# Context handed over transposed, half of the masks copied into PSUM by ScalarE, and a reordered rotary fill in a four-layer transformer kernel

## The chip, the core and the metric

The kernel runs on one core of one Trainium2 chip. The metric is the device time of one execution in microseconds (us). TensorE is called PE in the rows (PEld is its weight load), VectorE DVE, ScalarE ACT, GpSimd POOL; SyncE (SP) issues most DMAs.

## The reference, cut to what matters

`x` is [8, 256, 256] (8 sequences of 256 rows, 256 features), `ctx_1024` has the same shape. 16 heads of 16 features.

```python
def _layernorm(x): ...                      # no gain, no shift
x = x + tanh(g0) * L0_xattn(_layernorm(x), ctx, masks)   # two attention blocks
x = x + tanh(f0) * L0_ffn(_layernorm(x))                 # 8 experts, top 2
x = x + tanh(g1) * L1_xattn(_layernorm(x), ctx, keymask) # rotary cross attention
x = x + tanh(f1) * L1_ffn(_layernorm(x))                 # 8 experts, top 1

def mha(q, k, v, ..., mask):                # in L0_xattn: self, then on ctx
    att = Q @ K^T
    att = where(mask == 0, -1e9, att)
    att = softmax(att)
    return (att @ V) @ wo + bo
def L1_xattn(x, ctx):
    q, k, v = x @ Wq + bq, ctx @ Wk + bk, ctx @ Wv + bv
    q, k = rotary(q), rotary(k)
    return softmax(q @ k^T / 8 + keymask) @ v @ Wo + bo
```

## The kernel before, in words

The program has five stages, each a block of five instruction queues, one per engine, with all order between engines kept by semaphores: `prepare` (masks), `attention_pipeline` (both L0 attention blocks), `feed_forward_and_experts`, and `rotary_and_experts` (rotary attention, and its experts).

**Attention pipeline.** A unit `m` is one sequence in one of the two blocks: `m` = 0 to 7 is self attention, 8 to 15 attends to the context (`cross(m)`). The stage runs in beats `b` from -4 to 16, each of 16 slots `h`. In slot `h` of beat `b` PE computes the transposed scores of head `h` of unit `b` (`scores_T`, L523), the plain scores of a later head (`scores`, L505, from which DVE takes the row maxima in `maxima`, L761) and one task of another unit: queries in slot 0, keys in 4, value projection in 8, output projection in 12 (eight matmuls each), the product with V in 1, 5, 9 and 13 (`values`), small transposes in 3, 6, 7, 10, 11 and 15. In slot 14 of beats 4 to 11 `turn_context` (L468) transposes 256 rows of the context with four matmuls against the identity, and ScalarE copies the result to `cT` (`bring_context`, L612). Keys and values of a cross unit are made from `cT`.

Transposed scores use two PSUM banks, T0 for even heads and T1 for odd ones. Per head `scores_T` waits until ScalarE has taken the exponentials out of that bank two heads ago, and then issues three matmuls:

```python
pe.wait_ge(exp_done, H * m + h + 1)
nc.tensor.matmul(dst[:, :], identb[:, :], masks[m // B][1][:, :], start=True, stop=False)   # L528
for u in range(NU):                                                                         # L530
    ins = nc.tensor.matmul(dst[:, u * SEQ:(u + 1) * SEQ], KS[...], QS[...], start=False, stop=(u == NU - 1))
```

The first writes the mask (512 columns, bf16) into the bank, the others add the scores. ScalarE then runs `exps` (L646), an exponential of 128 x 512 from PSUM into `PT`. Between these, ScalarE's queue holds, in the order of the slots: `first_part` and `second_part` (queries and keys are split into three bf16 parts; GpSimd makes the remainders), `keys`, three copies of transposes, and `outputs`.

**Rotary stage.** It opens with a fill, written out by hand per engine, before its first beat. For units 0, 1, 2: transposed context, keys, values, transposed rows, queries; each result passes through one of two shared PSUM banks A and B in the order of the tuple `FILL` and is released by the engine that reads it. DVE multiplies by cosine and sine and leaves two halves in `fk`/`tk` or `fq`/`tq` (`turned`, L1786). GpSimd adds the halves (`whole`, L1632, 1635), and then ScalarE and GpSimd split the sum in turns (L1493, L1640, L1498, L1645). SP writes the parts to DRAM (`spread_parts`, L1080) and reads them back as stacked heads (`stack`, L1069) with the key mask. The rows `x` of a sequence need a layer norm first: DVE takes moments (L114, L118), GpSimd an inverse square root in 14 small steps (`inverse_roots`, L134 to L141), DVE scales (L151).

SP's order: rows of sequence 0, context 0, `wk`, `bk`, two key tables, `wv`, `bv`, the key mask `mcu` (2048 elements of one byte), `wq`, `bq`, two query tables, context 1 and 2, the constant stack rows, then all other `x`. DVE's order: memset of `V`, moments 0, keys 0, norm 0, moments 1, queries 0, keys 1, norm 1, queries 1, keys 2. Unit 2's rows and queries come in the last beat of the fill, b = -1, between the maxima of 8 + 16 heads. Then beat 0 starts with `scores_T(0, 0)` (L1241), which waits for the maxima of unit 0 that SP copies into `QS` (`max_to_queries`, L1084, 1085). In beats 0 to 3, slot 14, the context of unit b + 4 is transposed here too (L1181).

## Time and profile before

| | us |
|---|---|
| median of 3 runs | 1367.42 (1365.85 to 1368.43) |
| the profiled execution's own time | 1368.68 |
| its span, first to last instruction | 1366.9 |
| PE busy | 1199.9 (88%) |
| DVE / ACT / POOL busy | 781.0 / 569.9 / 556.7 |
| from the first `scores_T` of the attention pipeline to its last | 72.2 to 435.4 |
| rotary fill: first DMA issue to first `scores_T` | 887.2 to 964.6 |

Busy time of PE contains the latency of pipelined matmuls: of two that start 0.22 us apart each is shown as 0.38 us long. What one costs in a full queue is the distance between starts.

### The profile page before, as it was taken

The numbers are of one execution on the slowest core, as the hardware profiler recorded it, in microseconds if no ns is written. First come the engines' busy times: TensorE is split into PE (matmuls) and PEld (weight loads), VectorE is DVE, ScalarE is ACT, GpSimd is POOL, SyncE is SP. The second block draws the span as 40 slices with busy tenths as digits, with TensorE's granted clock in tenths as the row PEclk, the third lists the DMA queues.
The fourth block names the chain that finished last, engine by engine and source line by source line (L and its number), as shares of the span: only waits on it lengthen the run. The fifth ranks groups of instructions, "written<-read, shape, count | busy, mean of one in ns | idle before, by whom it ended". The sixth has DMA issues, their size and how long they took to land. (4 is left out here: it accounts for less than half of the span.)

```text
span 1366.9 us, 27489 instructions
## 1 busy us (share of the span) xinstructions
PE 1199.9 (88%) x8469; PEld 968.4 (71%) x8524; DVE 781.0 (57%) x2994; ACT 569.9 (42%) x1404; POOL 556.7 (41%) x927
## 2 busy tenths in 40 slices
PE   4599999999998999899999999447888868689996
PEld 3367677777755788789999999434556645689995
DVE  4587777777773378865333333136787876532231
ACT  2156566666655223233333333112455545233331
POOL 3334454453534235545333333144554433433331
PEclk9799999999999999999999999876899999799998
DMA  4766664635420991123222222187453695511110
GB/s 107 167 139 161 140 162 101 121 84 110 101 48 2 304 285 33 47 30 46 32 40 40 36 37 35 17 188 162 105 105 86 144 279 186 186 33 46 40 35 6
DMA packets 116679, 137.66 MB, mean 101 GB/s; under 512 B 25627, under 2 KB 102953, under 8 KB 111628
## 3 DMA queue, kind: packets, MB, share of 16 engines
q1 hardware_dynamic: 101304, 106.73, 33.1%
q0 software_dynamic: 15232, 29.17, 9.3%
q8 instruction: 72, 1.18, 0.4%
q14 instruction: 71, 0.58, 0.2%
HBM read 102.51 MB, written 35.97 MB: 101 GB/s over the span
## 5 line engine op out<-in xcount | busy, mean ns | idle before, releaser
L768 DVE CUSTOM_DVE_ANT_0 att_masked_scores<-att_S,Bm 128x256 bf16<-128x256 f32 x512 | 192.4, 419 | 66.9 <-PE att_S L511 52.8
L648 ACT ACTIVATE att_PT<-att_T 128x512 f32<-128x512 f32 x256 | 151.4, 595 | 86.3 <-PE att_T L530 77.6
L2432 ACT ACTIVATE moe_hT<-moe_H,moe_b 128x128 f32<-128x128 f32 x312 | 89.2, 369 | 170.1 <-PE moe_H L2345 168.9
L2357 PE MATMUL moe_Z<-moe_W,moe_hT 128*128 x624 | 141.6, 380 | 0.8 <-DVE moe_z L2657 0.8
L2520 POOL DMA_INDIRECT x<-Y,X x39 | 63.7, 1634 | 154.7 <-DVE Y L2668 150.4
L2357 PEld LDWEIGHTS moe_Z<-moe_W,moe_hT 128*128 128x128 f32 x624 | 115.5, 190 | 15.5 <-issue 1.2
L511 PE MATMUL att_S<-L_KS,L_QS 96*128 96x256 bf16 x512 | 99.7, 277 | 18.3 <-DMA L_KS<-att_k_dram 13.3
L530 PE MATMUL att_T<-L_QS,L_KS 99*128 99x256 bf16 x512 | 98.6, 273 | 4.6 <-issue 2.1
L2345 PEld LDWEIGHTS moe_H<-moe_aT,ff_w 128*128 128x128 f32 x832 | 96.8, 192 | 4.0 <-issue 2.1
L2345 PE MATMUL moe_H<-moe_aT,ff_w 128*128 128x128 f32 x832 | 97.2, 275 | 2.3 <-DVE X L2652 1.7
L1805 DVE TENSOR_REDUCE out_mx<-out_S 128x2 f32<-128x512 f32 x128 | 85.1, 684 | 24.6 <-PE out_S L1223 24.0
L2657 DVE TENSOR_TENSOR moe_z<-moe_Z,moe_b 128x256 f32<-128x256 f32 x39 | 16.5, 424 | 141.8 <-PE moe_Z L2357 141.8
L1551 ACT ACTIVATE X<-out_T,L_b 128x128 f32<-128x128 f32 x184 | 52.5, 369 | 98.1 <-PE out_T L1352 97.7
L1352 PEld LDWEIGHTS out_T<-out_xT,L_w1s 128*128 128x128 f32 x736 | 87.2, 195 | 4.4 <-issue 1.8
L1352 PE MATMUL out_T<-out_xT,L_w1s 128*128 128x128 f32 x736 | 87.9, 279 | 2.6 <-DVE L_w1s L1946 1.4
L1517 ACT ACTIVATE L_W<-out_T 128x512 f32<-128x512 f32 x128 | 72.5, 596 | 34.0 <-PE out_T L1241 33.5
L1365 PE MATMUL out_S<-L_W,X 128*128 x368 | 83.5, 380 | 2.4 <-DVE out_ys L1955 2.4
L530 PEld LDWEIGHTS att_T<-L_QS,L_KS 99*128 99x128 bf16 x512 | 50.6, 99 | 38.6 <-issue 0.6
L528 PE MATMUL att_T<-BmT,identb 128*128 128x512 bf16 x201 | 77.2, 384 | 0.4
L1365 PEld LDWEIGHTS out_S<-L_W,X 128*128 128x128 f32 x368 | 68.1, 190 | 11.8 <-issue 3.5
L511 PEld LDWEIGHTS att_S<-L_KS,L_QS 96*128 96x128 bf16 x512 | 48.3, 98 | 32.6 <-DMA L_KS<-att_k_dram 14.2
L1223 PE MATMUL out_S<-L_W 97*128 97x256 bf16 x256 | 52.8, 293 | 21.1 <-DVE out_mx L1805 13.1
(455 smaller groups left out, 2527.1 us busy)
## 6 DMA issues: line engine op xcount, KB each, us to landing
moe_W<-in_L_ffn_W SPq DMA_DIRECT2D x16, 1024.0 KB, 13.6
L_W<-in_L_ffn_W POOLq DMA_DIRECT2D x12, 1024.0 KB, 10.7
att_q_dram<-att_pq SPq DMA_DIRECT2D x16, 384.0 KB, 4.5
att_k_dram<-att_pk SPq DMA_DIRECT2D x16, 384.0 KB, 2.8
L_QS<-att_q_dram SPq DMA_DIRECT2D x16, 384.0 KB, 4.9
L_KS<-att_k_dram SPq DMA_DIRECT2D x16, 384.0 KB, 8.1
L_QS<-att_q_dram SPq DMA_DIRECT2D x16, 256.0 KB, 5.6
L_KS<-att_k_dram SPq DMA_DIRECT2D x16, 256.0 KB, 8.5
```

The source lines that it names most:

```text
L511: ins = nc.tensor.matmul(bankS[h % 2][:, u * SEQ:(u + 1) * SEQ], QS[0:ROWS, m % 3, h, u * P:(u + 1) * P], KS[0:ROWS, m % 3, h, :], start=T ...
L528: nc.tensor.matmul(dst[:, :], identb[:, :], masks[m // B][1][:, :], start=True, stop=False)
L530: ins = nc.tensor.matmul(dst[:, u * SEQ:(u + 1) * SEQ], KS[0:ROWS_ALL, m % 3, h, u * P:(u + 1) * P], QS[0:ROWS_ALL, m % 3, h, :], start=Fa ...
L648: nc.scalar.activation(PT[:, h % 8, :], bankT[h % 2][:, :], ACT.Exp).then_inc(exp_done, 1)
L768: ins = nc.vector.tensor_tensor_reduce(masked_scores[:, h % 2, u, :], bankS[h % 2][:, u * SEQ:(u + 1) * SEQ], masks[m // B][0][:, u * SEQ: ...
L1352: ins = nc.tensor.matmul(bankH[half][:, f * P:(f + 1) * P], matrix[:, cc, k * P:(k + 1) * P], xT[:, s % 2, cc * P:(cc + 1) * P], start=(cc ...
L1365: ins = nc.tensor.matmul(bankY[:, 0:D], eT[:, s % 2, f * P:(f + 1) * P], matrix[:, f, :], start=(f == 0), stop=(f == NF - 1))
L1517: nc.scalar.activation(PT[h % 8], bankT[h % 2][:, :], ACT.Exp).then_inc(exp_done, 1)
L1805: nc.vector.tensor_reduce(mx[:, m % 2, :, h:h + 1], bankS[h % 2][:, :].rearrange("p (u k) -> p u k", u=NU), AXX, ALU.max).then_inc(max_don ...
L2345: ins = nc.tensor.matmul(bankH[half][:, f * P:(f + 1) * P], matrix[:, cc, g * P:(g + 1) * P], xT[:, s % 2, cc * P:(cc + 1) * P], start=(cc ...
L2357: ins = nc.tensor.matmul(bankZ[:, 0:D], eT[:, s % 2, f * P:(f + 1) * P], w2e[:, f, :], start=(f == 0), stop=(f == NF - 1))
L2432: ins = nc.scalar.activation(eT[:, s % 2, g * P:(g + 1) * P], bankH[half][:, f * P:(f + 1) * P], ACT.Relu, bias=b1[:, bass.ds(e * NF + g, 1)])
```

## The change

Three things change together.

1. The host hands over `ctx_1024` with its last two axes exchanged. `turn_context`, `bring_context`, `cT` and the bank task "c" go away in both stages; keys and values are made straight from the loaded tile `C`. The load of the attention pipeline becomes eight DMAs, one per sequence, in place of one; `keys` waits for all of them.
2. In the attention pipeline the mask of odd heads is no longer written by PE. ScalarE copies it into bank T1 (`seed`) after each odd exponential, and the two score matmuls add to it. Only head 1 of unit 0 and all even heads keep the mask matmul.
3. The rotary fill takes another order: per unit keys, rows, queries, values for units 0, 1 and 2, all ahead of the maxima. The inverse roots of sequences 0 to 3 and the sums of the rotated halves of units 0 to 2 are made by DVE. The memset of `V` moves to GpSimd. The value weights, `bv` and `mcu` are loaded after the query weights, tables and stack rows; the rows of sequences 2 to 4 are loaded between the stacks; those of 5 to 7 after them.

```diff
+QUICK_STEPS = 8
+def quick_roots(nc, dve, t, q, moments, quick_step, n):
+    base = QUICK_STEPS * n
+    def after(i, ins):
+        ins.then_inc(quick_step, 1)
+        dve.wait_ge(quick_step, base + i)
+    dve.wait_ge(moments, 2 * n + 2)
+    after(1, nc.vector.tensor_scalar(t["ve"][:, :], t["mv"][:, :, 1], EPS, None, ALU.add))
+    nc.vector.tensor_scalar(q["less"][:, :], t["ve"][:, :], -0.5, None, ALU.mult)
+    after(2, nc.vector.tensor_scalar(t["guess"][:, :], t["ve"][:, :].bitcast(I32), -0.5, HALF_ROOT, ALU.mult, ALU.add))
+    r, i = t["guess"][:, :].bitcast(F32), 2
+    for k, out in enumerate((q["r"][0], q["r"][1], t["r"][2])):
+        for u in range(NU):
+            ins = nc.vector.scalar_tensor_tensor(q["some"][:, u:u + 1], r[:, u:u + 1], q["less"][:, u:u + 1], r[:, u:u + 1],
+                                                 ALU.mult, ALU.mult)
+        after(i + 1, ins)
+        after(i + 2, nc.vector.scalar_tensor_tensor(out[:, :], q["some"][:, :], 1.5, r, ALU.add, ALU.mult))
+        r, i = out[:, :], i + 2
...
 def load_context(sp, mem):
-    sp.dma_start(mem["C"][:, :, :], mem["ctx_in"].rearrange("b (u p) d -> p (b u) d", p=P)).then_inc(mem["c_in"], 16)
+    for n in range(B):
+        sp.dma_start(mem["C"][:, n, :, :], mem["ctx_in"][n].rearrange("(c p) t -> p c t", p=P)).then_inc(mem["c_in"], 16)
...
             def scores_T(m, h):
                 if h == 0:
                     pe.wait_ge(max_rows[m % 3], 32 * (m // 3 + 1))
-                pe.wait_ge(exp_done, H * m + h + 1)
                 dst = bankT[h % 2]
-                nc.tensor.matmul(dst[:, :], identb[:, :], masks[m // B][1][:, :], start=True, stop=False)
+                if h % 2 and (m, h) != (0, 1):
+                    pe.wait_ge(seeded, seed_no(m, h))
+                else:
+                    pe.wait_ge(exp_done, H * m + h + 1)
+                    nc.tensor.matmul(dst[:, :], identb[:, :], masks[m // B][1][:, :], start=True, stop=False)
...
+            def seed(m, h):
+                act.wait_ge(exp_done, H * m + h + 3)
+                layer = (m if h + 2 < H else m + 1) // B
+                nc.scalar.activation(bankT[1][:, :], masks[layer][1][:, :], ACT.Copy).then_inc(seeded, 1)
...
                         exps(b, h)
+                        if h % 2 and (b, h) != (M - 1, H - 1):
+                            seed(b, h)
...
+READY = 3
+FILL = tuple((k, m) for m in range(READY) for k in ("k", "x", "q", "v"))
+LAST_FILL = {9: (("m", 0),), 12: (("x", 3),)}
...
 # SP, rotary
             load_sums(0)
-            load_rotary(sp, mem)
+            load_rotary(sp, mem)      # context 0, key weights and tables, query weights and tables, stack rows
-            for n in range(1, B):
-                load_sums(n)
-            for m in range(2):
+            load_sums(1)
+            load_context_of(sp, mem, 1)
+            load_values(sp, mem)      # wv, bv, mcu
+            for m in range(READY):
                 spread_parts(m, 1)
                 stack(m, 1)
+                if m + 2 < B:
+                    load_sums(m + 2)
+                    if m == 0:
+                        load_context_of(sp, mem, 2)
                 spread_parts(m, 0)
                 stack(m, 0)
+            for n in range(READY + 2, B):
+                load_sums(n)
             (router weights)
             load_rest(sp, mem)        # contexts 3 to 7, wo, bo
             max_to_queries(0)
...
 # PE, rotary fill
+            for m in range(READY):
+                keys(m)
+                turn_rows(m)
+                queries(m)
+                project_values(m)
 # ACT, rotary fill
+            for m in range(READY):
+                bring_rows(m)
+                split(m, 1)
+                split(m, 0)
+                value_rows(m)
 # POOL, rotary fill
+            nc.gpsimd.memset(V[:, :, :, :], 1.0).then_inc(ready0, 1)
+            for m in range(READY):
+                for side in (1, 0):
+                    rest(m, side)
+                    third_part(m, side)
 # DVE, rotary fill
+            def whole(kind, m, f, other):
+                dve.wait_ge(*taken(kind, m))
+                nc.vector.tensor_tensor(f[:, :], f[:, :], other[:, :], ALU.add).then_inc(f_sum["qk".index(kind)], 1)
+            for m in range(READY):
+                input_moments(m)
+                input_norm(m)                 # quick_roots for n <= READY
+                if m == 0:
+                    dve.wait_ge(mem["k_in"], 16 * 4)
+                turned_keys(m)
+                whole("k", m, fk, tk)
+                if m == 0:
+                    dve.wait_ge(mem["q_in"], 16 * 4)
+                queries(m)
+                whole("q", m, fq, tq)
+                if m == 0:
+                    dve.wait_ge(mem["v_in"], 16 * 3)
+                    nc.vector.tensor_copy(mcf[:, :], mem["mcu"][:, :]).then_inc(kept_in, 1)
```

## Rows read from the trace of the kernel before

**Rows 1.** Windows: stretch, its length, busy us of each engine, PE clock, DMA share, GB/s.

```profile
72.00:436.00 364.00, 355.84 (x2915) 250.34 (x2970) 269.49 (x1343) 226.50 (x432) 164.43 (x348) 1.00 0.50 109
872.00:964.00 92.00, 44.21 (x153) 29.45 (x153) 38.03 (x84) 14.03 (x25) 35.60 (x84) 0.67 0.69 149
```

**Rows 2.** Waits, 72 to 436 us: total us, times, longest.

```profile
ACT att_PT L648 <- PE att_T L530: 77.6, 82, 3.1
```

**Rows 3.** Timeline of PE, beat 10: start, us, instruction.

```profile
333.14 0.38 PE L528 MATMUL att_T<-BmT,identb 128*128 128x512 bf16 x1
...
339.70 0.38 PE L528 MATMUL att_T<-BmT,identb 128*128 128x512 bf16 x1
339.92 0.38 PE L530 MATMUL att_T<-L_QS,L_KS 99*128 99x256 bf16 x2
340.14 0.38 PE L511 MATMUL att_S<-L_KS,L_QS 96*128 96x256 bf16 x2
340.36 1.89 PE L483 MATMUL att_B<-att_cT,L_wk 128*128 128x256 f32 x8
...
356.83 0.60 PE L474 MATMUL att_B<-ident,L_C 128*128 128x128 f32 x4
357.27 0.38 PE L528 MATMUL att_T<-BmT,identb 128*128 128x512 bf16 x1
```

**Rows 4.** Timeline of ACT, same beat.

```profile
346.86 0.63 ACT L643 ACTIVATE att_pk<-att_rk 128x512 bf16<-128x512 f32 x1 [0.56 <-POOL att_rk L690]
347.40 0.58 ACT L648 ACTIVATE att_PT<-att_T 128x512 f32<-128x512 f32 x1
```

**Rows 5.** Groups by line: busy us, mean ns of one, idle before.

```profile
L648 ACT ACTIVATE att_PT<-att_T 128x512 f32<-128x512 f32 x256 | 151.4, 595 | 86.3 <-PE att_T L530 77.6
L638 ACT ACTIVATE att_pk<-att_fk 128x512 bf16<-128x512 f32 x16 | 10.2, 638 | 0.1
L1845 DVE SCALAR_TENSOR_TENSOR X<-out_z,gates,X 128x512 f32<-128x512 f32 x8 | 6.0, 752 | 0.3
```

**Rows 6.** Timeline of all engines, rotary fill.

```profile
891.22 0.23 POOL L134 TENSOR_SCALAR out_xve<-out_xmv 128x2 f32<-128x2 f32 x1 [15.59 <-DVE out_xmv L118]
891.77 3.29 SPq L939 DMA_DIRECT2D L_W<-in_c_L_wq  x1
894.00 3.78 PE L1190 MATMUL out_B<-L_W 128*128 128x256 f32 x8 [2.06 <-DMA L_W<-in_c_sink]
894.85 0.20 POOL L141 TENSOR_TENSOR out_xr<-out_xr,out_xc 128x2 f32<-128x2 f32 x1
899.55 1.68 DVE L151 TENSOR_SCALAR Y<-X,out_xmv,out_xr 128x256 f32<-128x256 f32 x2
909.19 0.75 DVE L114 BATCH_NORM_STATS2 out_xstats<-X 128x6 f32<-128x256 f32 x2 [7.96 <-DMA X<-x]
934.96 0.60 PE L1223 MATMUL out_S<-L_W 97*128 97x256 bf16 x4
936.20 6.36 DVE L1805 TENSOR_REDUCE out_mx<-out_S 128x2 f32<-128x512 f32 x10
956.54 0.53 SPq L1084 DMA_DIRECT2D L_W<-out_MT  x1
964.56 0.64 PE L1241 MATMUL out_T<-L_W 99*128 99x256 bf16 x2
```

**Rows 7.** Windows of one microsecond in the fill, columns as in rows 1.

```profile
893.00:894.00 1.00, 0.00 (x1) 0.00 (x1) 0.00 (x0) 0.00 (x0) 0.69 (x4) 0.50 1.10 354
903.00:904.00 1.00, 1.00 (x6) 0.90 (x5) 0.00 (x0) 0.10 (x1) 0.82 (x1) 1.00 1.40 120
```

**Rows 8.** One line in the fill: duration in ns, min/median/max.

```profile
L151 DVE TENSOR_SCALAR Y<-X,out_xmv,out_xr x8: 400/424/1356, 899.6 to 961.0; 128x256 f32<-128x256 f32 x8
```

**Rows 9.** Timeline of DVE: dependent one-column instructions.

```profile
868.27 0.17 DVE L2662 RECIPROCAL moe_wt<-moe_wt 128x1 f32<-128x1 f32 x1
868.47 0.16 DVE L2663 SCALAR_TENSOR_TENSOR moe_wt<-X,moe_wt 128x1 f32<-128x1 f32 x1
```

**Rows 10.** DMA issues of the fill: KB each, median us from issue to landing.

```profile
X<-x SPq DMA_DIRECT2D x8, 256.0 KB, 10.7
L_W<-out_MT SPq DMA_DIRECT2D x2, 8.0 KB, 2.6
```

More of the change, by code:

```diff
@@ L119, in row_moments, with inverse_roots @@
     ins.then_inc(moments, 1)
-def inverse_roots(nc, pool, t, moments, root_step, n):
-    base = ROOT_STEPS * n
+def inverse_roots(nc, pool, t, moments, root_step, n, first=0):
+    base = ROOT_STEPS * (n - first)
     def after(i, ins):
@@ L145, in inverse_roots, with quick_tiles @@
     return last
+QUICK_STEPS = 8
+def quick_tiles(sb):
+    return {"less": sb("less", [P, NU]), "some": sb("bent", [P, NU]), "r": [sb(f"qr{i}", [P, NU]) for i in range(2)]}
+def quick_roots(nc, dve, t, q, moments, quick_step, n):
[15 more added lines that the diff above has]
+        r, i = out[:, :], i + 2
 def normal_rows(nc, x, y, t):
@@ L261, in shared_banks @@
                 unit = QUADS * b + off if kind == "o" else b + off
-                if 0 <= unit < (QUADS * M if kind == "o" else M) and (kind != "c" or crossed(unit)):
+                if 0 <= unit < (QUADS * M if kind == "o" else M):
                     bank = sum(used) % 2
@@ L466, in turn_rows @@
                 ins.then_inc(filled("x", m), 1)
-            def turn_context(m):
-                pe.wait_ge(mem["c_in"], 16)
-                pe.wait_ge(*free("c", m))
-                dst = bank_of("c", m)
-                for cc in range(NC):
-                    for u in range(NU):
-                        ins = nc.tensor.transpose(dst[:, cc * SEQ + u * P:cc * SEQ + (u + 1) * P],
-                                                  here(C, m)[:, u, cc * P:(cc + 1) * P], ident[:, :])
-                ins.then_inc(filled("c", m), 1)
             def product(kind, m, wt, src):
@@ L596, in _ @@
                         project_out(b - 1)
-                    if h == 14 and has(b + 4) and cross(b + 4):
-                        turn_context(b + 4)
                     if h in TURN_AT and 0 <= turning < QUADS * M:
@@ L610, in bring_rows @@
                 nc.scalar.activation(flat(xT[:, :, :]), bank_of("x", m)[:, :], ACT.Copy).then_inc(emptied("x", m), 1)
-            def bring_context(m):
-                if m >= 1 and cross(m - 1):
-                    act.wait_ge(*full("v", m - 1))
-                act.wait_ge(*full("c", m))
-                nc.scalar.activation(flat(cT[:, :, :]), bank_of("c", m)[:, :], ACT.Copy).then_inc(emptied("c", m), 1)
             def bring_heads(m):
@@ L678, in _ @@
                         bring_rows(b + 4)
-                    if h == 14 and has(b + 4) and cross(b + 4):
-                        bring_context(b + 4)
                     g = QUADS * b + (h - 5) // 4
@@ L951, in load_rotary @@
     table("sink", mem["k_in"])
-    matrix("wv", mem["v_in"])
-    columns("bv", mem["v_in"])
-    sp.dma_start(mem["mcu"][:, :], mem["keys"].rearrange("b (u p) -> p (b u)", p=P), allow_slow_non_contiguous=True).then_inc(mem["v_in"], 16)
     matrix("wq", mem["q_in"])
@@ L1202, in keys @@
                     pe.wait_ge(mem["k_in"], 16 * 4)
-                pe.wait_ge(*taken("c", m))
-                product("k", m, w["wk"], cT)
+                pe.wait_ge(mem["c_in"][m], 16)
+                product("k", m, w["wk"], C[m])
             def project_values(m):
@@ L1385, in _ @@
                 scores(*scores_of(-1, h))
-                if h == 2:
-                    turn_rows(2)
-                if h == 5:
-                    queries(2)
                 if h == 9:
@@ L1418, in _ @@
                         project_out(b - 1)
-                    if h == 14 and has(b + 4):
-                        turn_context(b + 4)
                     if b == M - 1 and h == 11:
@@ L1597, in _ @@
                         bring_rows(b + 4)
-                    if h == 14 and has(b + 4):
-                        bring_context(b + 4)
                     quad = QUADS * b + (h - 5) // 4
@@ L1695, in first_expert @@
             def first_expert():
-                pool.wait_ge(*full("c", M - 1))
+                pool.wait_ge(*full("k", M - 1))
+                pool.wait_ge(*full("v", M - 1))
                 load_expert(pool, 0)
```

130 lines of the change are left out of this document (32 added, 98 removed).

## The prediction, made before the changed kernel was built or run

> **What bounds the kernel now.** I read the windows by stage first. In the attention pipeline PE is busy 355.8 of 364 us at full clock, DVE 269 and ACT 227 [rows 1]; in the table of waits the largest entry there is ACT waiting for PE, 77.6 us [rows 2]. So this stage is as long as PE's queue, and a matmul taken out is worth the distance between starts. The rotary fill is the opposite: PE is busy 44 of 92 us, its mean granted clock is 0.67, that is partly the lower of its two levels, and no engine is full [rows 1]. It is a chain of waits through all five queues, so I followed the timeline there [rows 6], then DMA rates and landings [rows 7, 10]. The two expert stages are not touched, and I give them nothing.
>
> **Masks.** The start of the mask matmul and that of the next are 0.22 us apart (339.70, 339.92) [rows 3]. There are 128 odd heads, one keeps its mask: 127 x 0.22 = 27.9 us off PE's queue, 1.76 us for each of 16 beats.
>
> The cost is a wait. ScalarE gets 127 copies of 128 x 512. No row shows a copy from SBUF into PSUM; the nearest are the exponential from PSUM (0.595) and the copy within SBUF (0.638) [rows 5]; I take 0.60 and keep 0.5 and 0.75 as bounds. It starts only when its own exponential has ended, where a following one could overlap it (starts 0.54 apart for a length of 0.63 [rows 4]), so a seed adds some 0.65 to ScalarE: 5.2 us a beat on 14.2 (226.5 over 16), 19.4 in a beat of about 22.5. ScalarE has the room on average; two banks don't let it work ahead. For T1 the loop from one pair of score matmuls to the next is 0.38 (the pair) + 0.60 + 0.60 + some 0.12 for three signals = 1.70. Between them PE has 1.10 (five groups of 0.22) plus the tasks of two slots. With eight matmuls (1.73) or a V product (about 1.0) among them that is over 2 in every pair of a full beat: the loop alone never holds PE. What does is ScalarE's queue order. I walked through one beat, times from its first mask matmul, PE's slots with the distances of before less 0.22 in odd slots:
> - slot 1: scores at 2.4, exponential 2.8 to 3.4, seed 3.45 to 4.05, `first_part` from 3.95, `outputs` to 4.8, so the exponential of slot 2 ends at 5.4. PE wants bank T0 for slot 4 at 5.25: it waits 0.2.
> - slot 5: `keys` end at 8.8, exponential, seed, `first_part`, `outputs` to 10.9, exponential of slot 6 to 11.5. PE wants slot 8 at 11.1: 0.4.
> - slot 7: `second_part` waits for GpSimd, as before (0.56 idle) [rows 4], and the exponential of slot 8 starts some 0.5 later than now. Slot 8 holds a projection, which hides it. Slots 9 to 15: none late by more than 0.05.
>
> A full beat gives 1.76 - 0.6 = 1.15 us; 13 of the 16 are full: 15.0. In the last three the projections of new units are missing and three pairs of odd slots have only one 0.22 task between them: 1.32 against 1.70, 0.38 each, so 0.6 stays of 1.76: 1.9. Together 17 of 27.9. DVE works 0.70 per head and would be next; in the walk its maxima are done at least 0.1 us before PE needs the bank.
>
> A rule of the Trainium skill bears on the price. The exponential that reads PSUM and writes SBUF takes 0.595 and no row writes to PSUM from ScalarE [rows 5]. "ScalarE: Activation LUTs", step by step, says that ScalarE writes to PSUM with less latency than to SBUF. No run here shows it; by the rule the seed would be below 0.60, and by the row it is 0.60, where the sum stands.
>
> **Context.** Four transposes take 0.44 (356.83 to 357.27), so a beat with them is 24.13 long (333.14 to 357.27) [rows 3]. Eight beats of the pipeline: 3.5 us, all on PE's path. ScalarE's eight copies go too. The load turns from one issue into eight of about half a microsecond on SP in beat 1, behind the maxima of unit 2; what is queued behind them is the stack of unit 4, needed ten microseconds later: nothing. In the rotary beats 0 to 3 the four transpositions are at most 1.8; PE is not full there; I take 1.
>
> **The fill, in steps** [rows 6]. Today T(0,0), the first `scores_T`, starts at 964.6. In the new order:
> - Rows 0 land by 890 as now; DVE norms at once. Its roots are eight dependent steps of 0.20 [rows 9] plus four overlapped: 1.9 us against 3.8 on GpSimd (891.2 to 895.05). Rows 0 are normed at 894 instead of 901.2, where DVE now comes to them only after keys 0.
> - Keys 0 start at 894.0 as now, waiting for the sine table, and take 3.8 at the low clock. Rows are turned behind them, queries 0 start at about 899.7 instead of 902.7; `wq` no longer sits behind the byte-wise `mcu`, whose burst holds its issue for 3.3 us. The sum of halves on DVE: 0.75 for two SBUF inputs [rows 5] against 1.27 on GpSimd after a signal. Keys' first part is ready near 900.3, queries 0 at 904.
> - Then a new wait. DVE waits for `mcu` before moments 1, and PE's values 0 stand in front of keys 1. `mcu`, `wv`, `bv` and rows 1 now follow the stack rows. While those were moving, the engines were 1.4 busy at 120 GB/s, against 354 before [rows 7], for some six microseconds. The bytes up to `mcu` are 2.9 MB from 889: 7 us for the first 2.1 MB, 6 for the stack rows, 3 for the rest and 2 for the burst come to 907. So DVE goes on at about 907, not 904.4. Today it stood still until 909.2 for rows 1 [rows 6].
> - Unit 1 takes 11.5 us from there on DVE (moments 1.1, roots and norm 2.9, keys, sum, wait for queries, queries, sum): 918.7. Unit 2 the same: its queries' sum at 930.5. Scores of unit 0 start near 929 instead of 935, maxima near 931 instead of 936.2.
> - From the first maximum to T(0,0) it is now 28.4 us. DVE's work there will be 24 maxima x 0.66, moments of 3 and 4 2.2, norm 3 2.7, small maxima steps 1.6: 22.3, of which 1.3 is behind T(0,0): 21. What goes is rows and queries of unit 2 and two waits for GpSimd's roots. 931 + 21 = 952.
> - SP now has rows 5 to 7, contexts 3 to 7, `wo` and `bo`, ten large DMAs, between the last stack and `max_to_queries(0)`. Issues end near 945.4, when the maxima are ready too, but 2.4 MB are then in the queues. Such a copy landed in 2.6 us; rows queued among their like took 10.7 [rows 10]. I add 2.5: T(0,0) at 954.5, a gain of 10. Bounds: 3 (the last copies late by 10.7, `mcu` at 909) and 15 (`mcu` at 904.4, no backlog).
>
> Rows scaled by DVE took 1.36 us each at most and 0.40 at least [rows 8]. The Trainium skill has a rule for this ("SBUF — State Buffer", on the shared port pair): a DVE instruction in its two-port mode, or with two SBUF inputs, and one of GpSimd exclude each other for their whole length. The spread of that line agrees. The six new sums on DVE are of the second kind; by the rule each could be held up to one GpSimd instruction.
>
> **The sum.** 17 + 3.5 + 1 + 10 = 31.5 us. The profiled execution took 1368.7 (span 1366.9 and 1.8 around it); that is 1.3 above the median. 1368.7 - 31.5 = 1337.2, against the median 1336.
>
> **The rivals.**
> - *Full yield* (0.12): the seeds cost less than I think and the two waits vanish: 27.9 + 3.5, and a fill of 12: 44 us, 1323. For it: ACT's 77.6 us of waiting [rows 2]. Against: the queue order above.
> - *The two banks bind harder* (0.22): a seed of 0.75, and DVE's maxima, due 0.1 us before PE needs them, late. Each odd pair then loses another 0.1: half of the 17 is gone. 8 + 3.5 + 1 + 10: 1345.
> - *The fill gives it back* (0.20): `mcu` late, the ten DMAs in front of the maxima's copy, DVE's sums held by GpSimd. 17 + 3.5 + 1 + 3: 1343; with the rival before 1352.
> - *Slower* (0.03): ScalarE becomes the bound of the pipeline. Its beat is 14.2 + 8 x (seed + 0.05); the old 23.9 is passed at a seed of 1.16 us, and the other gains of 14.5 over 13 full beats are eaten at 25.0, a seed of 1.3. At 1.5 it would be 1388. Against it: both neighbours are half of that [rows 5].
> - *Does not do what it says* (0.03): gains meet losses within 0.2% (2.7 us, about what a measurement of this kernel can tell from no change).
>
> My forecast has 0.40. Its own range is 1329 to 1342. The range for 8 in 10 goes from the full yield to both losses together: 1322 to 1353. Faster by over 0.2%: 0.94; within: 0.03; slower: 0.03.
>
> **What would show it.** L528 falls to 129 matmuls; a beat of the pipeline is about 22.5 us; the stage from first to last `scores_T` falls from 363 to about 343; seeds last 0.5 to 0.65; PE waits for exponentials of slots 2 and 6, not for seeds. In the fill: norm 0 near 893, DVE held by `mcu` until about 907, first scores near 929, T(0,0) near 954. I am wrong if PE waits for seeds in every beat, if DVE becomes the one that PE waits for, or if T(0,0) starts before 949 or after 961.

## The result and the profile after

The changed kernel takes 1352.53 us (median of 4 runs, 1350.61 to 1355.98) where the kernel before, run beside it, takes 1367.93: a ratio of 0.9896, 95% interval 0.9873 to 0.9920. It is faster, by some 15 us. The forecast was 31.5 us and 1336, its own range 1329 to 1342: the time lies outside that, at the upper end of the wide range (1322 to 1353), and less than half of the gain came.

I cut both profiled executions at the same events, the first and last start of the `scores_T` matmuls in each stage and the first context load of the rotary stage (view of one line: shortest, median and longest duration in ns, then first and last start in us). After:

```profile
L561 PE MATMUL att_T<-L_QS,L_KS x512: 270/272/421, 70.9 to 424.9; 99*128 99x256 bf16 x171
L1268 PE MATMUL out_T<-L_W x256: 269/273/421, 952.3 to 1140.8; 99*128 99x256 bf16 x128
L961 SPq DMA_DIRECT2D L_W<-in_c_ctx x8: 434/469/1222, 876.7 to 944.5; - x8
```

The same views of before give 72.4 to 435.4, 964.6 to 1155.1 and 887.7. So the 14.9 us between the spans (1366.9 and 1352.0) are: first `scores_T` 1.5 earlier, attention pipeline 363.0 to 354.0 (9.0), the stretch of the experts 0.5, rotary fill 76.9 to 75.6 (1.3), rotary beats 190.5 to 188.5 (2.0), the end 0.6. Each is a comparison of two single executions, good to a few us: the first 1.5 is not shown to come from the change (`before_with_loads`, below, starts its first `scores_T` at 70.5 too). Forecast: 20.5 in the attention pipeline, 10 in the fill, 1 in the rotary beats. The attention pipeline and the fill are missing 20 us between them.

Windows of the two stretches that answer to [rows 1]:

```profile
71.00:425.00 354.00, 341.02 (x2807) 231.54 (x2805) 274.82 (x1338) 285.53 (x550) 163.62 (x348) 0.98 0.51 111
876.00:952.00 76.00, 39.03 (x138) 24.07 (x138) 48.29 (x169) 12.24 (x22) 20.05 (x36) 0.68 0.84 181
```

Groups of ScalarE by line in the first of them, with idle time before:

```profile
L672 ACT ACTIVATE att_PT<-att_T 128x512 f32<-128x512 f32 x256 | 146.5, 591 | 52.9 <-PE att_T L561 49.1
L677 ACT ACTIVATE att_T<-BmT 128x512 f32<-128x512 bf16 x127 | 76.4, 601 | 4.0
```

A seed lasts 601 ns, ScalarE went from 226.5 to 285.5 us of work and still waits 49 us for PE [rows 2]. The mean clock is 0.98 where it was 1.00 [rows 1]: that is new, and it is a trace of what went wrong.

A full beat is as forecast. Once a beat PE transposes the row maxima of a unit (`att_MQ`); I call these the turned maxima and measure beats from one to the next. The timeline of PE where those of two units start, 22.57 us apart, against 24.13 in [rows 3]:

```profile
340.37 0.23 PE L548 MATMUL att_A<-identb,att_MQ 128*32 128x128 bf16 x1
...
362.94 0.23 PE L548 MATMUL att_B<-identb,att_MQ 128*32 128x128 bf16 x1
```

and inside such a beat:

```profile
331.16 0.38 PE L583 MATMUL att_B<-ident,att_OTS 128*128 128x128 f32 x2
331.52 0.39 PE L559 MATMUL att_T<-BmT,identb 128*128 128x512 bf16 x1
...
336.78 0.38 PE L539 MATMUL att_S<-L_KS,L_QS 96*128 96x256 bf16 x2
337.00 0.39 PE L583 MATMUL att_A<-ident,att_OTS 128*128 128x128 f32 x2
337.44 0.39 PE L559 MATMUL att_T<-BmT,identb 128*128 128x512 bf16 x1
```

Before, the mask matmul started 0.22 after such a turned output (the next row is the 339.70 of [rows 3]):

```profile
339.48 0.38 PE L551 MATMUL att_A<-ident,att_OTS 128*128 128x128 f32 x2
```

Here the distance is 0.36 and 0.44. These are the waits of slots 4 and 8 for the exponentials of slots 2 and 6: 0.14 and 0.22 (walked: 0.2 and 0.4). A third, 0.20, stands before one pair of scores (347.82 to 348.24, where 0.22 is usual), which I take for a wait for DVE's maxima. In all the beat lost 0.64 of the 1.76 us of masks, where I had 0.6, and the context's 0.44 came whole: 1.12 + 0.44 = 1.56.

So the loss is in other beats. I list, for every pair of neighbouring turned maxima (15 intervals), the distance in us, worked out from the PE timelines:

```
interval        1     2     3     4     5     6     7   8 to 13 each  14    15
before        18.3  22.0  24.0  24.5  23.7  24.1  24.1   24.1        20.4  19.5
changed       21.9  21.4  23.5  26.3  22.4  24.3  22.4   22.6        19.7  19.3
```

Interval 1 of before is a lucky one: in `before_with_loads`, which does not touch it, it is 21.2, so the 9.0 us of the stage may be up to 3 too few. Interval 4 got longer. The timeline of PE there and three windows of two microseconds:

```profile
152.18 0.38 PE L561 MATMUL att_T<-L_QS,L_KS 99*128 99x256 bf16 x2
154.28 0.61 PE L539 MATMUL att_S<-L_KS,L_QS 96*128 96x256 bf16 x2 [1.72 <-DMA L_KS<-att_k_dram]
154.69 3.35 PE L530 MATMUL att_B<-L_wv,att_xT 128*128 128x256 f32 x8
```

```profile
152.00:154.00 2.00, 0.56 (x3) 0.16 (x3) 1.90 (x8) 1.93 (x4) 1.42 (x3) 1.00 0.56 151
154.00:156.00 2.00, 1.72 (x6) 1.39 (x7) 1.06 (x6) 0.66 (x2) 1.15 (x1) 0.56 0.06 17
156.00:158.00 2.00, 2.00 (x8) 1.52 (x7) 0.00 (x0) 0.00 (x0) 0.00 (x0) 0.59 0.67 197
```

Read it in this order: PE stands 1.72 us for the stacked keys of the next unit; right after that idle time the granted clock is at about half, the 1.2 GHz level; and the value product behind it takes 3.35 us where eight such matmuls take 1.89 at the upper level. The low level is there too from 69 to 75.5 us (interval 1); interval 6 has a wait of 1.57 for stacked keys and no low clock. A fourth wait for stacked keys, 1.81, ends at 381.85, in interval 14, and the clock falls behind it, into interval 15:

```profile
384.00:386.00 2.00, 2.00 (x12) 1.02 (x8) 0.59 (x3) 0.92 (x2) 1.27 (x1) 0.50 0.04 8
```

Before has the same there, a wait of 2.16 and the low level behind it, so this one is no loss against before, but it is time to be won.

The fill, lines from the timelines of DVE, PE and SP: the two waits for the key mask, the copy that makes the maxima ready, SP's queue, and T(0,0):

```profile
896.89 0.17 DVE L1970 CAST out_mcf<-L_mcu 128x16 f32<-128x16 uint8 x1 [2.38 <-DMA L_mcu<-in_mask_BxS_bf]
...
896.91 1.22 PE L1240 MATMUL out_B<-L_W 128*128 128x256 f32 x2 [5.35 <-DMA L_mcu<-in_mask_BxS_bf]
...
936.38 0.27 DVE L1813 COPY out_MT<-out_A 32x256 bf16<-32x256 bf16 x1
...
937.88 1.25 SPq L1103 DMA_DIRECT2D L_W<-out_q_dram  x3
939.18 1.45 SPq L1138 DMA_DIRECT2D X<-x  x3
...
941.69 3.44 SPq L961 DMA_DIRECT2D L_W<-in_c_ctx  x5
945.17 0.91 SPq L1003 DMA_DIRECT2D L_wo<-in_L_xattn_Wo  x1
...
946.64 0.53 SPq L1118 DMA_DIRECT2D L_W<-out_MT  x1
...
952.32 0.61 PE L1268 MATMUL out_T<-L_W 99*128 99x256 bf16 x2 [8.60 <-DMA L_W<-out_MT]
```

The maxima were ready at 936.6, their copy was issued ten microseconds later, behind the last stack and the loads, and PE stood 8.6 us at T(0,0).

### The profile page after: what moved, and what is told of

It reads as the page before. It is cut to its first block and busy times, and to the rows that moved or that the text cites. A ratio compares the mean times of both kernels' runs of the same rounds, so it can differ in the third digit from the quotient of the medians.

```text
span 1352.0 us, 27241 instructions
## 1 busy us (share of the span) xinstructions
PE 1182.9 (87%) x8333; PEld 944.0 (70%) x8333; DVE 797.2 (59%) x3047; ACT 624.9 (46%) x1515; POOL 539.8 (40%) x866
## 3 DMA queue, kind: packets, MB, share of 16 engines
q8 instruction: 70, 1.15, 0.4%
## 5 line engine op out<-in xcount | busy, mean ns | idle before, releaser
L672 ACT ACTIVATE att_PT<-att_T 128x512 f32<-128x512 f32 x256 | 146.5, 591 | 52.9 <-PE att_T L561 49.1
L1797 DVE TENSOR_REDUCE out_mx<-out_S 128x2 f32<-128x512 f32 x128 | 84.7, 685 | 31.6 <-PE out_S L1250 30.8
L677 ACT ACTIVATE att_T<-BmT 128x512 f32<-128x512 bf16 x127 | 76.4, 601 | 4.0
L1392 PEld LDWEIGHTS out_S<-L_W,X 128*128 128x128 f32 x368 | 68.1, 190 | 11.8 <-issue 3.5
L575 PE MATMUL att_O<-att_PT,att_V 128*32 128x256 f32 x1024 | 70.2, 388 | 0.7 <-ACT att_PT L672 0.7
## 6 DMA issues: line engine op xcount, KB each, us to landing
moe_W<-in_L_ffn_W SPq DMA_DIRECT2D x16, 1024.0 KB, 13.5
```

The lines of the kernel that those rows point to most:

```text
L672: nc.scalar.activation(PT[:, h % 8, :], bankT[h % 2][:, :], ACT.Exp).then_inc(exp_done, 1)
L677: nc.scalar.activation(bankT[1][:, :], masks[layer][1][:, :], ACT.Copy).then_inc(seeded, 1)
L1392: ins = nc.tensor.matmul(bankY[:, 0:D], eT[:, s % 2, f * P:(f + 1) * P], matrix[:, f, :], start=(f == 0), stop=(f == NF - 1))
L1797: nc.vector.tensor_reduce(mx[:, m % 2, :, h:h + 1], bankS[h % 2][:, :].rearrange("p (u k) -> p u k", u=NU), AXX, ALU.max).then_inc(max_don ...
```

## The experiments

Twelve kernels, each timed beside the kernel before in its own series; ratios are to it. Stage times are of the one profiled execution, cut as above. Two kernels of one series can be told apart by their times to some 4 us (their two 95% intervals together), so where a difference of 6 to 9 us is read below, its size rests on the lengths of the intervals in the profiles, and its sign on both.

```
kernel                     us      ratio (95% interval)      attention  fill   rotary beats
before                                                       363.0      76.9   190.5
changed                  1352.5   0.9896 (0.9873 - 0.9920)   354.0      75.6   188.5
after_again              1353.7   0.9913 (0.9890 - 0.9935)   349.5      74.7   188.3
no_seeds                 1362.1   0.9964 (0.9946 - 0.9983)   360.6      74.2   188.8
loads_behind_stack       1347.1   0.9868 (0.9847 - 0.9890)   345.9      75.0   187.9
maxima_first             1346.1   0.9864 (0.9841 - 0.9887)   346.8      67.8   188.2
double_seed              1376.8   1.0073 (1.0045 - 1.0101)   376.1      75.0   191.5
three_moves              1337.8   0.9788 (0.9766 - 0.9809)   345.4      68.7   189.1
three_moves_warm         1337.3   0.9795 (0.9771 - 0.9818)   344.5      67.6   188.6
three_moves_late         1338.6   0.9795 (0.9772 - 0.9818)   344.7      68.1   190.5
three_no_seeds           1352.4   0.9887 (0.9867 - 0.9907)   358.5      67.1   190.2
before_with_loads        1368.5   0.9995 (0.9974 - 1.0017)   364.4      75.5   191.4
four_moves               1342.1   0.9812 (0.9794 - 0.9829)   346.4      65.6   194.4
four_moves_warm_fill     1341.4   0.9807 (0.9790 - 0.9823)   346.4      64.1   194.6
```

**after_again.** No edit.

> The changed kernel itself, beside which the next three are read. 0.9896 of the time before (about 1352.5 us); its profile should again show a beat of 22.6 us where nothing is in the way, two beats of the pipeline (the fourth and the sixth interval between the transpositions of the maxima) lengthened by waits for the stacked keys, and T(0,0) of the rotary stage 76 us after that stage's first load is issued. If the low clock in the first beat and in the fourth is chance, it will lie elsewhere here.

1353.7. Interval 4 is 24.06 long and interval 6 24.01. The waits for stacked keys are there (1.14 and 1.27), the low clock behind the first is not. Interval 1 is 20.4. The same kernel differs by 4.5 us in this stage between two executions, and its six runs go from 1347.6 to 1357.3. The waits are there in both executions; the low clock is not.

**no_seeds.** All odd heads:

```diff
-                if h % 2 and (m, h) != (0, 1):
-                    pe.wait_ge(seeded, seed_no(m, h))
-                else:
-                    pe.wait_ge(exp_done, H * m + h + 1)
-                    nc.tensor.matmul(dst[:, :], identb[:, :], masks[m // B][1][:, :], start=True, stop=False)
+                pe.wait_ge(exp_done, H * m + h + 1)
+                nc.tensor.matmul(dst[:, :], identb[:, :], masks[m // B][1][:, :], start=True, stop=False)
...
-                        if h % 2 and (b, h) != (M - 1, H - 1):
-                            seed(b, h)
```

> The changed kernel with all 256 mask matmuls on PE and no seed on ScalarE. My theory now: a seed is worth what the walk said only in the undisturbed beats (1.12 us each); in the others the seeds' gain is eaten by waits for stacked keys (and the low clock behind one of them), in the first and last beats by waits for the seeds themselves. Then seeds are worth some 7 us in all: about 1359.5 (1357 to 1362), full beats 23.7, the wait for stacked keys near the fourth interval back to 0.7 or less. Rival one, the sum of the prediction: 17 us, so 1369.5. Rival two, the seeds give nothing and the whole gain is from the context and the fill: 1352 to 1354.

1362.1, 8.4 (give or take 4) above the changed kernel of the same series: near my theory (7, at most 1362) and not the 17 of the sum. Full beats are 23.69 long, 0.44 less than before: the context's four transposes, no more and no less. PE's waits for stacked keys are 0.83 and 0.90 in intervals 4 and 6, a little over the 0.7 I expected, against 1.72 and 1.57, and 1.14 and 1.27, in the two executions with the seeds. What is left of the change without the seeds, context and fill together, is a ratio of 0.9964; no run separates these two.

**loads_behind_stack.**

```diff
                 if has(b + 2):
                     stack(b + 2)
+                if b >= 1:
+                    load_in_beats(sp, mem, X, *loads, b)
+                if b == 4:
+                    load_feed_forward(sp, *ff)
                 if has(b + 3):
...
-                load_in_beats(sp, mem, X, *loads, b)
+                if b < 1:
+                    load_in_beats(sp, mem, X, *loads, b)
```

> The changed kernel; in beats 1, 2 and 4 of the pipeline SP issues the context, the second layer's weights and the feed-forward loads right behind the stack of that beat, and not at the beat's end, just ahead of the next stack. My theory: the stacked keys come late in two beats (1.7 and 1.6 us of PE's waiting) because their copies stand behind those loads, and the first wait also costs 1.8 us of low clock; gone, the time falls by about 5 us, to 1347.5 (1346 to 1349), and the two beats are 22.6 and 22.6 long. Rival: the copies of a stack are themselves as long as half a beat, which has become shorter, so the waits stay whatever is in front: 1351 to 1353. Rival two: the loads now collide with the spread of the next unit's parts, the waits appear one beat on: 1352 or more.

1347.1, 6.6 less (give or take 4). Intervals 4 and 6 are 22.76 and 22.56. Intervals 3, 4 and 6 together, the ones behind the moved loads, last 68.4 us, against 74.1 and 72.1 in the two executions of the changed kernel: 3.7 to 5.7 us is what the profiles show. PE's waits between 95 and 380 us, total, times, longest: first of the changed kernel, then of this one.

```profile
PE att_S L539 <- DMA L_KS<-att_k_dram: 3.5, 3, 1.7
```

```profile
PE att_S L542 <- DMA L_KS<-att_k_dram: 1.1, 1, 1.1
```

The waits of intervals 4 and 6 are gone (1.72 and 1.57, and 0.22 in interval 3); the one left is in interval 14, where beats are shorter because projections are missing, and where before waited 2.2.

**maxima_first.**

```diff
+            max_to_queries(0)
             for n in range(READY + 2, B):
                 load_sums(n)
...
             load_rest(sp, mem)
-            max_to_queries(0)
```

> The changed kernel; in the rotary fill SP issues the copy of unit 0's maxima to the stacks ahead of rows 5 to 7, the router's weights, contexts 3 to 7, wo and bo instead of behind them. My theory: PE waited 8.6 us at T(0,0) for this copy alone, issued 10 us after the maxima were ready; T(0,0) now starts when the last scores of the fill are through DVE, 68 to 69 us after the stage's first load is issued instead of 76, and nearly all of it reaches the end: about 1345.5 (1344 to 1348). Rival one: the contexts and rows now come late and the rotary beats give it back: 1350 to 1353, T(0,0) early all the same. Rival two: the copy is not what PE waited for (the walk of the prediction has DVE's maxima end near the same time): T(0,0) at 74 to 76 and no gain.

1346.1, 7.6 less (give or take 4), with a fill of 67.8 instead of 75.6 and 74.7. SP in the fill:

```profile
931.94 1.25 SPq L1103 DMA_DIRECT2D L_W<-out_q_dram  x3
933.23 0.53 SPq L1118 DMA_DIRECT2D L_W<-out_MT  x1
...
934.44 1.61 SPq L1138 DMA_DIRECT2D X<-x  x3
```

Two small copies, moved ahead of loads that nobody needed yet, shorten the fill by 7 us, nearly half of what the whole change gave. T(0,0) starts at 938.87, 5.6 us after the first of them is issued, as in the changed kernel (5.7): what was won is the time of the issue, not of the landing.

**double_seed.**

```diff
-                nc.scalar.activation(bankT[1][:, :], masks[layer][1][:, :], ACT.Copy).then_inc(seeded, 1)
+                nc.scalar.activation(bankT[1][:, :], masks[layer][1][:, :], ACT.Copy).then_inc(seed_first, 1)
+                act.wait_ge(seed_first, H // 2 * m + h // 2 + 1)
+                nc.scalar.activation(bankT[1][:, :], masks[layer][1][:, :], ACT.Copy).then_inc(seeded, 1)
```

> The changed kernel with each seed made by two identical copies, one behind the other with a signal between them. The walk of the prediction has ScalarE's beat at 14.2 + 8 x (seed + 0.05), so with the seeds now at 0.60 it is 19.4 of 22.6. A second copy and its signal add 8 x 0.7 = 5.6: 25.0 a beat, ScalarE becomes what sets it, and the time is 13 x 2.4 = 31 us more and some 4 in the last beats: 1385 (1378 to 1392). Rival: ScalarE works from a stock of its own and has more room than the walk says: PE's waits grow only where they are, the beat stays under 23.6 and the time under 1368.

1376.8, 23 more and not 31; a full beat is 24.03, not 25.0. One beat of the changed kernel and one of this, in windows:

```profile
340.37:362.94 22.57, 22.48 (x188) 15.71 (x187) 18.56 (x91) 18.59 (x37) 11.10 (x22) 1.00 0.53 107
```

```profile
328.15:352.18 24.03, 22.91 (x184) 15.57 (x187) 17.88 (x91) 22.73 (x45) 11.08 (x22) 1.00 0.45 100
```

ScalarE's own work is 18.59 a beat, where my walk had 19.4 (it had not taken off the context's copy, 0.6 in half of the beats, and allowed 0.05 behind each seed). At 22.7 of 24.03 it is nearly full and PE now waits for it. The rival, room to spare, falls, and so does my size: at seeds of 0.6 ScalarE has four microseconds a beat left, not three.

**three_moves.** Both edits above, and `load_values` issued at the end of `load_rotary`, ahead of the rows for the stacks:

```diff
     table("sinq", mem["q_in"])
+    load_values(sp, mem)
     for k, rows in (("KS", ...
```

> The changed kernel with three orders of SP changed: loads of beats 1, 2 and 4 right behind the stack, unit 0's maxima ahead of the rest of the loads, and wv, bv and the key mask ahead of the rows for the stacks in the rotary fill. Alone the first gave 6.6 us and the second 7.6 against the changed kernel. If they are independent, as they lie in different stages, both give 14 together: 1339.5. The third: DVE waited 2.4 us for the key mask and PE 5.4 for it and the values; my theory is that the chain of units 1 and 2 comes forward by 2 us, T(0,0) to 66 us after the stage's first load: 1337.5 (1335 to 1340). Rival: the stack rows and the first stack now come later by what the key mask no longer does, and scores start no earlier: 1339.5 or more, T(0,0) at 68.

1337.8: the first two add up (14 expected, 15.9 measured across two series, good to some 4 us). The third gives nothing that shows: the fill is 68.7 against 67.8. The key mask came 2 us earlier, as DVE's line for it shows, but then units 1 and 2 wait, each for the queries' product at the lower clock level:

```profile
893.12 3.75 PE L1220 MATMUL out_A<-out_xT,L_W 128*128 128x256 f32 x8 [1.13 <-DVE L_W L1782]
...
906.63 3.75 PE L1220 MATMUL out_A<-out_xT,L_W 128*128 128x256 f32 x8 [1.13 <-DVE L_W L1782]
```

**three_moves_warm.** In the two beats before the first `scores_T`, behind each pair of score matmuls:

```diff
+                        if b < 0:
+                            nc.tensor.matmul(bankT[0][:, :], identb[:, :], masks[0][1][:, :], start=True, stop=True)
```

> The three moves, and in the two beats of the attention fill ahead of the first scores_T each pair of score matmuls is followed by one more mask matmul into the still unused bank T0, so that PE has fewer gaps while it waits for DVE's maxima. My theory: the low clock that fell on the first beat (its first interval 20.4 to 21.9 us in four runs, 18.8 in the luckiest) comes from PE's idle time ahead of it; with the filler the granted clock stays 1.00 from 60 to 76 us, the interval is 18.5 to 19, and the time is about 2 to 3 us below that of the three moves, with less spread from run to run. Rival: the clock falls at that place whatever PE did in the 10 us before: no change. Rival two: the filler, 0.43 us at the low clock, delays the scores and the fill: 2 us slower.

Windows of the three moves, then of this kernel, same stretch:

```profile
68.00:70.00 2.00, 1.11 (x8) 0.36 (x7) 2.00 (x13) 0.00 (x0) 0.00 (x0) 0.93 0.43 84
70.00:72.00 2.00, 1.78 (x8) 1.39 (x8) 1.97 (x13) 0.60 (x1) 0.40 (x2) 0.50 1.19 298
```

```profile
68.00:70.00 2.00, 1.84 (x12) 0.99 (x12) 2.00 (x12) 0.00 (x0) 0.00 (x0) 1.00 0.63 192
70.00:72.00 2.00, 2.00 (x12) 1.58 (x11) 1.86 (x12) 0.60 (x1) 1.00 (x6) 1.00 1.20 189
```

With PE busy 1.84 instead of 1.11 of two microseconds the clock stays up, and interval 1 is 18.74. The time, 1337.3, can't be told from 1337.8. The profile of before has 18.3 there and `maxima_first` 18.8, both without a filler: so the low clock at this place is not certain in either kernel, and one execution with the filler doesn't prove that the filler kept it away. This stays open; it is worth 1 to 3 us in a single execution.

**three_moves_late.**

```diff
+        by_seed = lambda m, h: h % 2 == 1 and (m, h) != (0, 1) and not (m >= M - 3 and h in (1, 5, 9))
```

(with the seeds' count and the mask matmul following `by_seed`).

> The three moves, and heads 1, 5 and 9 of the last three units keep their mask matmul on PE instead of a seed (9 of 127). There no projection stands between one odd head and the one before the seed, and PE waited 0.25 to 1.0 us for the seeds of these heads (3.7 us for seeds in all). My theory: each of these waits becomes 0.22: the stretch from the last turned maxima (unit 15's) to the last scores_T falls from 23 by some 2 us, the time by 2: 1335.5. Rival: PE waits for the exponential of the same head instead, since ScalarE's queue is what is late there: no change in time, waits moved from the seed's line to the exponential's.

In the profile as expected: PE's waits for seeds fell from 3.7 to 1.0 us, interval 15 from 17.77 to 17.32, and the stretch from unit 15's turned maxima to the last `scores_T` from 23.0 to 21.7, together 1.7. The time, 1338.6, doesn't resolve it: interval 14 (19.8 against 19.2) and the rotary beats (190.5 against 189.1) were longer in this execution.

**three_no_seeds.** The two edits of `three_moves` and `no_seeds` together.

> The three moves with all 256 mask matmuls on PE, to be read against the three moves (1337.8 us), where the stacked keys are late in one place only. My theory: the seeds lost 10 of their 17 us in the changed kernel to the waits for stacked keys and the low clock, not to a wrong size of a seed; here they are worth 1.12 in each of nine full beats, 0.5 to 1.1 in the first three and 0.5 in the last: 13 us, so 1351 (1349 to 1353). Rival: the seeds are worth about as much as against the changed kernel (8.4 us): 1346.

1352.4, ratio 0.9887 against 0.9788: 13.5 us, as my theory had it (13), and not 8.4. The two sizes, 8.4 and 13.5, are each good to 4 us, so the times alone hardly part them. The intervals do: over intervals 3, 4 and 6 the seeds are worth 2.9 us here (71.3 against 68.4), and with the loads in front 1.3 in one execution and less than nothing, -0.7, in the other (73.4 against 72.1 and 74.1).

**before_with_loads.** The edit of `loads_behind_stack` in the kernel before.

> The kernel before with only the loads of beats 1, 2 and 4 behind the stack. If the late stacked keys were exposed by the shorter beat, there is little to win here: PE waited 0.67 us for them in that stretch, so 1365.2 against 1365.8 (1363.5 to 1366): the same beats of 24.1. Rival: the move is worth 5 us or more for itself, and has nothing to do with the change: 1361 or less.

No change in time (0.9974 to 1.0017), interval 4 0.8 shorter. Over intervals 3, 4 and 6 the move is worth 0.8 us before the change and 3.7 to 5.7 after it: the longer beat had covered most of the lateness.

**four_moves.** The three moves, and one more place ahead for the maxima's copy:

```diff
                 spread_parts(m, 0)
+                if m == READY - 1:
+                    max_to_queries(0)
                 stack(m, 0)
```

> The three moves, and the copy of unit 0's maxima one place further ahead on SP: in front of the stacking of unit 2's queries, which had SP wait until 929.2 us for a copy while the maxima were ready at 927. My theory: T(0,0) had still 2.4 us of waiting for this copy; it starts 66.3 us after the stage's first load instead of 68.7, and the time is 2.4 less: 1335.4 (1334 to 1337). Rival: the copy was not ready earlier in any way that counts, since SP stands at the spread in front: T(0,0) at 68 and 1337.8.

A miss. T(0,0) came at 65.6, earlier still than expected (66.3), and the time is 1342.1, slower than three_moves (0.9812 against 0.9788; the intervals just overlap). The rotary beats took 194.4 instead of 189.1, and 4.4 of these 5.3 us lie between T(0,0) and the next turned maxima (20.4 against 16.0). In beat 0:

```profile
944.20 1.58 PE L1296 MATMUL out_O<-L_wo,out_bv_wide 128*128 128x256 f32 x4 [1.18 <-DMA L_bo<-in_L_xattn_bo]
```

PE now comes to the bias product before `bo` has landed, after 2.75 us of waits for DVE's maxima, and the granted clock falls to its lower level there for some microseconds (0.84 from 942 to 946, 0.73 from 946 to 950). The maxima of unit 1 are turned 85.9 us after the stage's first context load, in three_moves 84.7: what T(0,0) gained, beat 0 gave back and one more. The other 0.9 lies in later rotary beats, whose lengths differ by 0.6 to 1.6 us between the executions of these kernels in an order that I can't assign.

**four_moves_warm_fill.** The four moves, and filler matmuls in the rotary fill:

```diff
             for m in range(READY):
                 keys(m)
+                if m:
+                    fill_gap(6)
                 turn_rows(m)
+                fill_gap(3)
                 queries(m)
```

> The four moves, and in the rotary fill PE fills its gaps with matmuls of 512 bf16 columns into the unused bank T0: six behind keys 1 and 2, three behind each turning of rows. In the three moves PE did queries 1 and 2 at the low clock (3.75 us for eight matmuls against 1.97), DVE waited 3.2 us for each, and that wait ended last in both units. My theory: with the gaps filled the clock is at its full level there, each of these two waits becomes 1.4 us, first scores come 3.5 us earlier, and the time is 3.5 us below four_moves. Rival: the clock does not come back within this stretch of broken work, and the fillers, twice as long at the low level, stand in front of the turned rows: 1 to 3 us above four_moves.

1341.4 against 1342.1, no difference. T(0,0) is 1.5 earlier, and nothing of it reaches the end, as in four_moves. Queries 1 take 1.99 us where they took 3.75, so there the clock was at its upper level; queries 2 still take 3.65.

## Why the prediction was wrong

**Masks: the price per beat was right, the count of undisturbed beats was the step that failed.** "13 of the 16 are full: 15.0" holds for the beats where nothing else ends last; the walk's 1.15 a beat was 1.12. But I took the beat's other inputs as on time because they were on time before. SP issues a stack at the start of a beat, and the second half of that beat needs it. In the changed kernel, from 70 us on, the keys' copies landed 7.7 to 10.9 us after their issue:

```profile
DMA to landing us min/median/max: 7.7/8.7/10.9
```

From the issue of a stack's first key copy to the landing of its last it is 9.5 to 10.4 us in eleven stacks, and 11.8, 12.0 and 11.4 in the three behind the context, the second layer's weights and the feed-forward loads. The change moved the need forward: in interval 4 PE came to these keys 10.7 us after the first of these issues before, and 10.2 after. Before, PE waited 0.67 there; after, 1.72, and once more 1.57 behind the feed-forward loads; and behind the longer of these stands the clock fell in one of two executions (1.8 us more). `before_with_loads` shows that almost none of this cost existed without the change (0.8 us), `loads_behind_stack` that it is 3.7 to 5.7 us with it (6.6 by the medians), and `three_no_seeds` that with the loads out of the way the seeds give 13.5. I had looked at what is queued on SP behind the eight context loads and found nothing to pay; the stack behind them took 11.8 us, against 10.6 before, and PE waited 0.22 us for it, 0.74 in `after_again`. I had not looked at what every shorter beat does to copies whose own time stays the same.

**The low clock was not in the sum either.** With the loads moved and the clock up (`three_moves_warm`) the attention pipeline is 344.5 long, where I had 343. The changed kernel's 354.0 is 9.5 more: 5.3 in intervals 4 and 6 (late keys and the clock behind them), 2.3 between T(0,0) of this stage and the turned maxima of unit 1, and 1.8 in intervals 14 and 15, with the low level in parts of both stretches, 0.1 elsewhere. The profile of before has the low level until 63 us, ahead of the first `scores_T`, where PE waits for DVE's maxima anyway, and at 394 to 397 us.

**Last beats: 1.9 forecast.** Intervals 14 and 15 gave 0.9 together, with the clock low in a part of both kernels, and the stretch behind them lost 0.6 (22.4 to 23.0). PE waits 0.4 to 1.0 for each of four seeds there, where I had 0.38: the pair of score matmuls between two odd heads is missing in the last beat too. `three_moves_late` takes most of these waits away.

**Context: right.** 0.44 a beat, measured with and without seeds. The rotary beats gave 2.0, not 1.

**Fill: the step "Issues end near 945.4, when the maxima are ready too" failed.** Counted from the first context load (887.7 before), T(0,0) was to come at 66.8 and came at 75.6, that is 963.3 on the prediction's scale, past the 961 that it named as a sign of being wrong. SP's issues should have ended at 57.7; they ended at 69.9, because the last stack, which stands ahead of them, was issued at 61.2 (it waits until the parts have been written, 932.2 to 937.9), and the ten loads and the router's two took 7.5 more. The maxima themselves were ready at 59.9, 2.2 late. The rival that named the ten DMAs in front of the copy was what happened; I had given it 0.20. The landing itself, 5.7 us after the issue, was near my 2.6 + 2.5, but not for my reason: with none of the ten loads in front of it (`maxima_first`) the copy took as long. The sum had a slip too: 945.4 + 2.6 + 2.5 is 950.5, ahead of the 952 of DVE's work, so by its own terms the 2.5 added nothing. `maxima_first` puts the fill at 67.8, within 1 of the forecast, and that is in part luck: the first maxima started some 3 us late, and the needless 2.5 took most of it up. The key mask held DVE until 896.9 (907.9 counted as before), as forecast (907). Units 1 and 2 took 26.3 us instead of the 23.5 of the walk: DVE waited 3.3 us for queries 2, done at the lower clock level in 3.78 us. Norm 0 was on time.

**The rivals.** "Two banks bind harder" didn't occur in a full beat (0.64 lost against 0.6 walked), so that its 1352 together with the fill's loss is the measured time is chance: half of the missing pipeline gain went to late keys and clock, which no rival named. ScalarE as the bound appears only with the doubled seed (1.24 us for both copies and the signal). The "slower" rival had 1.16 us as the seed at which the old beat is passed and 1.3 for the whole gain. At 1.24 the kernel is 0.7% slower, but not by its full beats, which at 24.03 are still 0.1 under those of before: intervals 1 to 5 are 6.0 us longer together, the last two 1.5, and the stretch behind the last turned maxima 6.4 (28.8 against 22.4).

**A rule I weighed.** A seed takes 601 ns; the exponential from PSUM to SBUF 591. The Trainium skill ("ScalarE: Activation LUTs", step by step) gives PSUM as the faster destination; in the duration of the instruction these rows show no such gain.

## What to carry to other kernels

When a change shortens a stage that repeats, list every input that does not get faster with it (DMA copies, and the loads ahead of them in the queue) and set its time against the new period: a copy that was just on time is late now, and PE's idle time can cost as much again in clock (1.72 us of waiting and 1.8 behind it). On a hand-ordered DMA queue, put the small copy that somebody waits for ahead of large loads that nobody needs yet, but count what the delayed loads are needed for next: the first step gave 7.6 us, one more gave nothing or less. The best kernels measured, three_moves and its two variants, which the times can't tell apart, are 2.1% faster than before (three_moves: ratio 0.9766 to 0.9809), twice the change's own gain.

## What the runs showed of the hardware that I had not expected

- After 1.72 us in which PE stood still in an otherwise full pipeline, the granted clock was 0.56 and 0.59 for four microseconds; after 1.14 us at the same place, in another execution of the same kernel, it stayed 1.00. The other waits for stacked keys read the same way: it fell after 1.81, 1.97, 2.16 and 2.24 us (interval 14 of the changed kernel, `three_no_seeds`, before and `before_with_loads`), and stayed up after those of 1.65 us and less, and after 1.74 in `three_moves_late`.
- The six sums of halves on DVE in the fill (SBUF inputs) last 0.69 us where no GpSimd instruction runs, four times, and 1.15 and 1.22 us where a GpSimd subtraction with two SBUF inputs is under way when they start:

```profile
889.48 0.69 DVE L1785 TENSOR_TENSOR L_W<-L_W 128x512 f32<-128x512 f32 x1
893.37 1.15 DVE L1785 TENSOR_TENSOR L_W<-L_W 128x512 f32<-128x512 f32 x1
```

```profile
892.82 1.15 POOL L1637 TENSOR_TENSOR L_W<-L_W 128x512 bf16<-128x512 f32 x1 [0.75 <-ACT L_W L1503]
```

- A copy of ScalarE into PSUM, 512 columns from bf16, lasts 601 to 603 ns in all 127 cases.
